# Cross-attention and quantised feed-forward kernel: key product and x's transposes moved between scores and attended values, the update behind the masked queries

## The reference

```python
xn  = layernorm(x)
src = ctx @ W_src.T + b_src            # keys | values, both times the mask
q   = (xn @ W_tgt.T + b_tgt) * mask
p   = softmax(where(mask, q.k / 4, -inf))        # per head
x   = x + concat(xn, p @ v) @ W_out.T + b_out
xn2 = layernorm(x)
# fp4: blocks of 16, rounded to a grid by the block's largest magnitude
h   = silu(fp4(xn2) @ fp4(w_gate).T) * (fp4(xn2) @ fp4(w_up).T)     # width 352
out = x + fp4(h) @ fp4(w_down).T
```

## Time and profile before

| | |
|---|---|
| median of 3 runs | 202.84 us |
| lowest and highest | 201.23, 203.03 us |
| the profiled execution | 202.57 us |
| its span, first to last instruction | 200.3 us |
| granted TensorE clock, mean | 0.999 of full speed |
| busy: PE (TensorE matmuls) | 183.1 us, 91% |
| busy: DVE (VectorE) | 179.4 us, 90% |
| busy: POOL (GpSimd) | 142.3 us, 71% |
| busy: ACT (ScalarE) | 131.9 us, 66% |

### The profile page before, as it was taken

One profiled execution on the slowest core, in us unless ns is written; L12 is line 12 of the kernel. 1 busy time (PEld: TensorE's weight loads), 2 busy tenths in 40 slices (PEclk: granted clock), 3 DMA queues, 4 the chain that ended last, 5 costly groups with the idle time before them and its releaser, 6 DMA issues.

```text
span 200.3 us, 5826 instructions
## 1 busy us (share of the span) xinstructions
PE 183.1 (91%) x2097; PEld 140.8 (70%) x2097; DVE 179.4 (90%) x391; ACT 131.9 (66%) x280; POOL 142.3 (71%) x206
## 2 busy tenths in 40 slices
PE   5889998999799999999997998789999998999882
PEld 5565775859649788597885774567878675887781
DVE  6559999999999999979979879999999999999961
ACT  2076997959678699696968735485566564656750
POOL 6361893668898885955819575897999966868880
PEclk9999999999999999999999999999999999999999
DMA  5799970401100000000000000000101100110013
GB/s 194 250 236 369 365 233 5 157 5 44 64 3 2 3 3 3 2 0 3 5 3 0 3 2 0 0 2 5 52 0 56 43 10 0 56 39 17 0 52 108
DMA packets 13698, 11.99 MB, mean 60 GB/s; under 512 B 790, under 2 KB 10590, under 8 KB 13670
## 3 DMA queue, kind: packets, MB, share of 16 engines
q1 hardware_dynamic: 13086, 11.23, 17.9%
q10 hardware_dynamic: 584, 0.39, 0.6%
HBM read 9.52 MB, written 2.10 MB: 58 GB/s over the span
## 4 chain that ended last, share of the span: by engine, by line
PE 47%; POOL 18%; DVE 17%; issue 13%; ACT 2%; POOLq 0%; DVEq 0%; ACTq 0%
PE bank L1053 7%; PE bank L1144 5%; POOL wq_y L393 5%; PE bank L1041 4%; POOL hq L408 3%; PE bank L1112 3%; PE bank L1109 3%; PE bank L1124 3%; PE bank L1047 3%; POOL xn L284 3%; PE a_pair L1004 3%; DVE st L676 3%; PE bank L1016 2%; PE bank L1004 2%; DVE u L767 2%
## 5 line engine op out<-in xcount | busy, mean ns | idle before, releaser
L1144 PE MATMUL bank<-wdT,hT 128*128 128x128 f32 x186 | 26.4, 278 | 1.8 <-issue 0.8
L1109 PE MATMUL bank<-guT,xqT 128*128 128x352 f32 x64 | 24.6, 465 | 2.2 <-DVE hh L862 2.2
L1144 PEld LDWEIGHTS bank<-wdT,hT 128*128 128x128 f32 x186 | 23.2, 191 | 3.1 <-issue 1.9
L1112 PE MATMUL bank<-guT,xqT 128*128 128x352 f32 x64 | 24.2, 460 | 0.0
L408 POOL TENSOR_TENSOR hq<-wq_u,sch 128x704 f32<-128x704 f32 x15 | 21.2, 1413 | 3.7 <-DVE wq_u L888 3.5
L393 POOL TENSOR_TENSOR wq_y<-hh,ivh 128x704 f32<-128x704 f32 x15 | 21.1, 1407 | 3.4 <-ACT ivh L626 2.8
L732 DVE TENSOR_REDUCE den<-prob 128x8 f32<-128x512 f32 x32 | 19.8, 665 | 0.0
L620 ACT COPY hT<-bank 128x384 f32<-128x384 f32 x32 | 15.2, 473 | 5.1 <-PE bank L1124 5.1
L1053 PE MATMUL bank<-wsT,cT 128*128 128x128 f32 x128 | 17.0, 277 | 1.1 <-DVE q_m L706 1.1
L862 DVE TENSOR_TENSOR hh<-bank,mask_bc 128x352 f32<-128x352 f32 x32 | 15.9, 496 | 1.6 <-PE bank L1112 1.2
L1124 PE MATMUL bank<-ident,hq 128*128 128x128 f32 x96 | 15.9, 274 | 1.5 <-POOL hq L408 0.9
(11 more groups left out here) (138 smaller groups left out, 507.1 us busy)
## 6 DMA issues: line engine op xcount, KB each, us to landing
cT<-in_ctxT SPq DMA_DIRECT2D x8, 512.0 KB, 5.3
x_all<-in_x SPq DMA_DIRECT2D x8, 256.0 KB, 6.8
mask_bc<-in_mask_rows SPq DMA_DIRECT2D x8, 256.0 KB, 6.6
out_y<-mask_bc SPq DMA_DIRECT2D x7, 256.0 KB, 2.2
wsT<-in_WsT ACTq DMA_DIRECT2D x1, 256.0 KB, 4.8
out_y<-mask_bc SPq DMA_DIRECT2D x1, 192.0 KB, 2.0
w_all<-in_wg SPq DMA_DIRECT2D x1, 176.0 KB
w_all<-in_wu SPq DMA_DIRECT2D x1, 176.0 KB
```

The costliest lines, as they stand in the source:

```text
L1109: nc.tensor.matmul(gu_bank[2 * n % 3][:, 0:I], xqT[g % 2][:, t], guT[:, 0, :], start=True, stop=True).then_inc(pe_g, 1)
L1112: nc.tensor.matmul(gu_bank[(2 * n + 1) % 3][:, 0:I], xqT[g % 2][:, t], guT[:, 1, :], start=True, stop=True).then_inc(pe_u, 1)
L1144: last = nc.tensor.matmul(bank[:, j * P:(j + 1) * P], hT[n % 2][:, c, :], wdT[:, c, :], start=(c == 0), stop=(c == 2))
```

## The change

Three lists of `attn_step` change, for k from 2 to 7. On TensorE `k_project(g1)` and `xn_transpose(g1)`, in this order, now stand between `scores(g2)` and `attend(g3)`; they stood behind `spread_reciprocals(g3)`, in the other order. On ScalarE `k_evac(g1, 0)` and `xnT_evac(g1)` now stand ahead of `av_evac(g3)`; in step 2 the magnitudes of the weights stay behind `av_evac`, so the first key copy stands ahead of them now. On VectorE `update(g3)` goes from in front of `minus_max(g2)` to behind `q_masked(g1)`. Steps 0, 1 and 8 keep their order. No instruction is added or removed.

```diff
--- before.py
+++ after.py
@@ -570,15 +570,19 @@
                     k_evac(0, 0)
                     k_evac(0, 1)
                     normalise1(1)
+                if on(g1) and k > 1:
+                    k_evac(g1, 0)
+                if on(g1) and k > 0:
+                    xnT_evac(g1)
                 if on(g3):
                     av_evac(g3)
                 if on(g1) and k > 0:
-                    xnT_evac(g1)
                     if k == 2:
                         act.wait_ge(wy_ok, 1)
                         for b in w_halves:
                             nc.scalar.activation(wq_a[:, b, :], wq_y[:, b, :], ACT.Abs, scale=MAGIC).then_inc(wa_ok, 1)
-                    k_evac(g1, 0)
+                    if k == 1:
+                        k_evac(g1, 0)
                 if k == NG:
                     x0_evac()
                 if on(g2):
@@ -814,7 +818,7 @@
                 if on(g2):
                     for p in range(PAIRS):
                         row_max(g2, p)
-                if on(g3):
+                if on(g3) and k == NG:
                     update(g3)
                 if on(g2):
                     minus_max(g2)
@@ -826,6 +830,8 @@
                     weights_round_up()
                 if on(g1):
                     q_masked(g1)
+                if on(g3) and k < NG:
+                    update(g3)
                 if k == 1:
                     stats1(2)
                 if on(g2):
@@ -1160,6 +1166,9 @@
                     v_project(0, 0)
                     v_project(0, 1)
                     k_project(1)
+                if on(g1) and k > 1:
+                    k_project(g1)
+                    xn_transpose(g1)
                 if on(g3):
                     attend(g3)
                     spread_reciprocals(g3)
@@ -1170,10 +1179,8 @@
                     warm_up(8)
                     q_project(0)
                     warm_up(10)
-                elif on(g1):
+                elif k == 1:
                     xn_transpose(g1)
-                    if k > 1:
-                        k_project(g1)
                 if k == NG:
                     x0_transpose()
                 if on(g2):
```

## The result

The changed kernel takes 204.50 us (median of 7 runs, 203.08 to 205.74), the kernel before took 203.35 beside it on the same chip (7 runs, 201.23 to 205.19): a ratio of 1.0087 [1.0044, 1.013] with its 95% interval. The two medians are 1.15 us, 0.6%, apart; the ratio is taken from fast executions alone and not from these medians. So the changed kernel is slower by 0.6 to 0.9%, clear of no change and inside what I called the same.

The account below looks back on a forecast made before the run. TensorE was taken as full in steady steps, VectorE close behind. VectorE's 0.75 us from step 2 plus 0.55 per step, less waits for ScalarE, left 1.96 late: 202.57 + 1.96 = 204.5 us, range 204.0 to 205.2 (with rivals 202.4 to 205.9).

Parts of the forecast that it names:

- what I called the same: Whole time: within 1% of the kernel before, chance 0.50, against slower 0.42 and faster 0.08.
- What bounds the kernel: Steady steps: TensorE busy throughout, VectorE some 0.3 us behind; earlier masked queries can win only two waits, 1.1 us.
- the unnamed stall: Attend, start of step 4: 1.02 us, hidden by late queries; fourth rival, it moves to step 5 or later, 205.6, chance 0.13.
- The block maximum waits for xn2, 0.55 lost per step: VectorE, steps 3 to 7: block maximum moves up only 0.05 us, update then costs 0.60 in full, 0.55 more per step.
- TensorE's lateness at v_project: After v_project, steps 3 to 7: TensorE late by 0.56, 1.25, 1.55, 1.96 and 1.96 us.
- The slack method: At v_project: TensorE waits for query lateness beyond its slack, v_project's start less 0.06 hand-over less the queries' end.
- The sign that TensorE would wait for the queries: TensorE, steps 3 to 6: waits for the masked queries by 0.3 to 1 us if the forecast is right.
- Step 2: Late weight magnitudes make queries 0.15 us later; with the update's 0.60 behind, VectorE leaves the step 0.75 late.
- collision: Step 2: GpSimd's bias addition and VectorE's rounding block one another; without it, second rounding ends 0.28 us sooner, lateness 0.47.
- The first rival: Masked queries come 0.60 us earlier each step, both waits (0.7 in step 2, 0.40 in step 4) go: 201.5 us, chance 0.08.
- TensorE's order costs nothing, earlier exponentials gain nothing: TensorE and ScalarE: the four reordered pieces' sum is unchanged, cost 0; earlier exp cannot be used by prob's transposes, gain 0.
- The end of step 3 gives nothing back: GpSimd's product starts later too, so VectorE's lateness stays; second rival, it is taken back there: 203.2 us, chance 0.14.

Follow-up runs that it names:

- half of xn2: Changed kernel, GpSimd normalising two of four tiles for groups 0 to 5: 77.80 us from step 2's scores to step 8's (before 77.13, changed 78.80).
- block maximum last: Changed kernel with the block maximum behind the masked queries and the update in steps 3 to 7: 204.88 us, ratio 1.0102, stretch 78.63.
- Two experiments: Changed kernel with the update between subtraction and block maximum (stretch 77.81), and changed kernel with half of GpSimd's xn2 left out for six groups (77.80).
- VectorE's list alone: Kernel before with only the update moved behind the masked queries, TensorE and ScalarE in old order: 202.33 us, ratio 1.0001, stretch 77.74.
- the kernel with the best stretch: Kernel before, second half of step 2's rounding behind the masked queries, step 4's block maximum behind them too: 201.50 us, ratio 0.9996.

## Why the prediction was right

The time came as forecast, 204.5 us, by a sum that was right in its main mechanism, with one term too large and two small terms, of opposite sign, taken as nothing. The agreement to the last digit is luck: the forecast is 202.57 + 1.96, while the kernel before had 203.35 beside the changed one and the medians differ by 1.15; the start and the last store alone moved by more than the error. The stretch is the fair test, +1.67 for +1.96.

- *What bounds the kernel.* Held for steps 5 to 7. The 12.43 us of step 4 begin at 53.77, behind the unnamed stall; from scores to scores that step has 14.47, of which TensorE is busy for 13.05. Nothing was to be won behind earlier queries in a steady step: without the wait for xn2 they wait for q_project (half of xn2, block maximum last).
- *The block maximum waits for xn2, 0.55 lost per step.* Held. Two experiments take away the hole in opposite ways and both give 77.8: one us of the +1.67 is this. VectorE's lateness at the maxima (start after, less start before, less 0.81) was 0.73 in step 3, 1.26, 1.62, 1.79 and 1.58 in steps 4 to 7; I had 0.75, 1.30, 1.85, 2.24 and 1.96. **The term that was mis-sized** is the 0.55 at the end of steps 4 and 5: it grew by 0.36 and 0.17. I subtracted the wait for ScalarE only in step 5, by the 0.16 in the earlier trace rows. But step 4 had such a wait as well, which no row marks: before the change its rounding starts at 63.83, 0.03 behind the end of the magnitudes and 0.44 behind the start of the statistics' last operation (L681), after the change 0.30 behind that start, so 0.14 us were waiting. After the change no hold is left there at the end of steps 4 and 5, so VectorE had had more cover than the one row told.
- *TensorE's lateness at v_project.* 0.53, 1.20, 1.29, 1.48 and 1.66 in steps 3 to 7 against 0.56, 1.25, 1.55, 1.96 and 1.96. The slack method worked to 0.05 us until the mis-sized term came in. The sign that TensorE would wait for the queries by 0.3 to 1 us in steps 3 to 6 came in two of the four: 1.25 us in step 4, and in step 3 some 0.3 that no row marks (1.19 us from the transposes to v_project for 0.88). In steps 5 and 6 v_project starts 0.05 behind the queries' end and only its first half is longer, 1.00 us for 0.90.
- *Step 2.* Held in its sum, 0.73 of lateness for 0.75, by two errors that cancel: the magnitudes started 0.21 later than I had them (30.20 for 29.99), as attend stood 2.36 us later and not 2.16, and no collision followed, as the addition was nearly over when the roundings came. Less the 0.81 these ended at 32.79; I had 32.80. What I missed is that the step would have gained 0.75 without the late magnitudes. The first rival's part for step 2 was right, its part for step 4 (0.40) came only where the block maximum stood behind the queries.
- *TensorE's order costs nothing, earlier exponentials gain nothing.* **The step that failed**, by small sums: +0.20 us from scores to subtraction, -0.11 at the transposes of prob, +0.09 in a steady step. My reason for the first, that the sum of the four pieces is the same, took durations from one order into another. For the second I read that the transposes show no wait; their last four start 0.06 us behind the exponential that they read. And the cost without the moved update, which I had not worked out, is +3.20. TensorE's list alone, with all of ScalarE's as before, was not run.
- *The end of step 3 gives nothing back.* Held: the spreading of the reciprocals waits 1.04 us for VectorE instead of 0.47, and the product starts at 51.14, 1.27 later than before when the 0.81 is taken off, as late as the maxima of step 4.
- *The unnamed stall* did not move to another place; no wait of TensorE in attend is left. In step 4 a stall without a named cause (0.34 to 1.02 us, in one kernel 0.31 and 0.89) stands in all six kernels that have attend right behind the scores, and in none of the eight with k_project between. Step 4 is 15.04 us long with it (VectorE's list alone) and without it (the changed kernel). Late queries cover it there, as I had argued; in the kernel with the best stretch (76.37) it takes 0.75 us and no wait for the queries follows, so there it may cost time. What it is stays open.

Open as well: what makes operations longer where small and full matmuls meet, and whether the 0.76 us of the best stretch reach the time.

## What to carry to other kernels

A filler between two instructions that seem not to wait may be what hides a wait: before moving it, compare when the next operand is ready with when the next instruction starts, and if they are within 0.1 us, put something else in the hole. The same comparison finds waits that the profile does not mark: here 0.1 us per step at the transposes of prob and 0.14 at a rounding. When an operation is moved ahead of others, ask who reads those others' results, in all engines' lists: here attend's lateness would have cost 3.2 us, had the update not moved too. Differences below 1% are read from a stretch between two fixed instructions, step by step, not from whole times that also hold loads and stores.

## What was not expected of the hardware

- A change between small matmuls (32*64 or 128*32) and full ones on TensorE costs 0.05 to 0.11 us each, in longer durations and without a wait: 3.68, 3.70 and 3.73 us with one such place, 3.88 and 3.88 with three.
- Where GpSimd's bias addition and VectorE's two-input rounding meet, the order of arrival decides who pays: addition 1.92 us and both roundings 1.69 when it came during the second rounding, addition 1.94 and roundings 2.76 when it came during the first and slipped between them. The blocked instruction shows a longer duration and no wait; in both cases the addition ends 1.14 us behind the end of the rounding that ran when it started. The rule that the prediction cites from the Trainium skill ("SBUF — State Buffer", section "SBUF: two separate sides"), that the shared port pair is held for a whole instruction, fits both; which engine would get it first was for the runs to show.
- With the same list of loads and stores the first wait for x ended 1.2 us later in one of the two profiles, and the wait for the last store took 2.8 us in one and 1.2 in the other.
